# Bucket bits by two signs on ScalarE and a value bias by a one-row product, in a fused attention and feed-forward block

## The chip, the cores and the metric

One core of a Trainium2 chip runs the whole program in one launch. The metric is device time in microseconds, the median over runs; less is better.

## The reference

The input is 16 sequences of 512 tokens with 128 features. Each sequence goes through a layer norm, an attention with 16 heads of 8 features, a second layer norm and a residual, and then a feed-forward network with its own norm and residual. The attention compares queries with queries, and its scores are multiplied by 62, or by 63 where both tokens fall into the same bucket:

```python
q = (x @ Wq.T + bq).reshape(B, S, H, Dh)
v = (x @ Wv.T + bv).reshape(B, S, H, Dh)
proj = einsum('bshe,en->bshn', concat([q, ones]), hyperplanes)   # 6 numbers per token and head
bits = (proj >= 0)
buckets = einsum('bshn,n->bsh', bits, 2 ** arange(6))
scores = einsum('bhsd,bhtd->bhst', q, q) / sqrt(128)
coeff = 62 + (b_hs[:, :, :, None] == b_hs[:, :, None, :])
attn = softmax(scores * coeff)
out = einsum('bhst,bhtd->bhsd', attn, v)
# then: x = x + layernorm(out)
h = silu(x1 @ w1 * s1) * (x1 @ w2 * s2)      # 512 wide
h = gelu(h @ h1 * s3); h = gelu(h @ h2 * s4)
x = x + layernorm(h @ w3 * s5)
```

## The kernel before

The kernel works in turns. A turn i handles the attention of sequence i, and beside it the projections (q, buckets, v) of sequence i+1, the input norm of sequence i+2, and the feed-forward network of sequence i-1 and the end of that of i-2. Turns 2 to 13 carry all of this; turns 0 and 1 have no feed-forward end, turn 14 has no input norm, turn 15 no projection either. Sequence 0's projection stands ahead of turn 0, in a turn of its own without attention.

A turn has 64 slots, one for each attention tile (16 heads by 4 blocks of 128 tokens, 128 by 512 scores each). Every engine walks through the same 64 slots in its own program, and tables of numbers at the head of the file (`BITS_SLOT = 26`, ...) say in which slot of each engine's program a step stands. Each engine runs its program strictly in order and waits on semaphores. So a slot number is a place in an engine's queue, not a time.

A tile goes this way. TensorE multiplies the stacked query parts into one of four score banks (L550). VectorE makes the coefficients of the next tile (L758) and multiplies the scores with the present ones into a ring of 48 tiles in SBUF, with the row maximum beside it (L808). After 8 tiles (a group) VectorE transposes the maxima (L768), and SyncE's queue stores them to DRAM and loads them back as rows on all partitions. GpSimd subtracts the group's logits from them in one instruction of 128 by 4096 (L980), ScalarE takes the exponential in four instructions (L1032), and TensorE multiplies values and probabilities (L570), which for a quad of 16 tiles stand in slots 36 and 38 counted from the quad's first tile. The product of the turn's first quad, in slot 36, is called "the slot-36 product" below. A score product in slot k waits until VectorE is through with tile k-4.

The steps of the change, in before: TensorE projects the queries on the hyperplanes (slot 25, L606). VectorE adds the hyperplane bias and compares with 0, which gives bits of 0 and 1 in bf16 (slot 26, L880). TensorE weighs them with powers of two, once per token (slot 28, L612, copied by ScalarE at L1086) and once as a row (slot 37, L630, copied by ScalarE at L1095). TensorE makes the values in PSUM with four products (slot 32, L619), and VectorE adds the bias, which was loaded as 128 by 512, and writes them to `v_pad` (slot 32, L870). All of these share the bank `aux_bank` with the probability products, so the slot-36 product waits for `v_added` too. ScalarE also writes the first norm of the attention output (L1043, slot 31), for which VectorE waits at L896, and the SiLU (L1150), for which VectorE waits at L907.

## Time and profile before

| | before |
|---|---|
| median of 3 runs | 1383.29 us (1378.63 to 1386.29) |
| profiled execution, first to last instruction | 1378.0 us |
| TensorE busy | 1223.5 us, 89% |
| VectorE busy | 1225.7 us, 89% |
| ScalarE busy | 1084.6 us, 79% |
| GpSimd busy | 1221.7 us, 89% |
| mean granted TensorE clock | 0.975 |

Of the profiled execution only its span is known, 1378.0 us; the fastest of the three runs is 0.6 us above it and the median 5.3 us. Three engines are busy for the same share, so the shares alone don't tell which of them sets the pace: that is read from what ends last in each turn. In this trace a turn is cut at a small memset that VectorE makes in its last slot (L805).

### The profile page before, as it was taken

The page shows a single profiled execution, that of the slowest core. Times are in us where ns is not written, and L with a number is a line of the kernel's source. Part 1 is how long each engine was busy: PE and PEld are TensorE (multiplying, and loading weights), DVE is VectorE, ACT ScalarE, POOL GpSimd, SP SyncE. Part 2 cuts the span into 40 slices and gives each one's busy share as a digit, 9 for nine tenths or more (in the row PEclk, how much of TensorE's full clock was granted, in tenths as well). Part 3 has the DMA queues.
Part 4 walks back from the last instruction along what each step waited for, and adds up shares of the span by engine and source line. Part 5 has one row for each costly group of instructions (what it writes and reads, how often), then busy time and mean ns, then how long its engine had stood idle before and what let it go on. Part 6 is the DMA issues. An engine that isn't in the chain of part 4 may idle for free. (4 is left out here: it accounts for less than half of the span.)

```text
span 1378.0 us, 19641 instructions
## 1 busy us (share of the span) xinstructions
PE 1223.5 (89%) x5302; PEld 500.2 (36%) x5394; DVE 1225.7 (89%) x3837; ACT 1084.6 (79%) x1573; POOL 1221.7 (89%) x259
## 2 busy tenths in 40 slices
PE   3666799999989999998989999998999999898897
PEld 1211234343333434333343434433343433333343
DVE  4988999999999999999999999999999999999420
ACT  2344778979797988979798897979798897979852
POOL 2699999999999999999999999999999998999810
PEclk9877999999999999999999999999999999999998
DMA  3563445444544455455544544454454535453100
GB/s 104 154 182 112 132 111 154 127 130 120 147 120 118 132 134 141 109 140 125 131 133 124 142 123 132 133 139 129 114 136 128 145 98 146 120 135 102 40 8 8
DMA packets 89470, 167.37 MB, mean 121 GB/s; under 512 B 18192, under 2 KB 54160, under 8 KB 89360
## 3 DMA queue, kind: packets, MB, share of 16 engines
q1 hardware_dynamic: 89252, 165.82, 44.6%
q8 instruction: 43, 0.70, 0.2%
q14 instruction: 67, 0.55, 0.1%
q10 hardware_dynamic: 108, 0.30, 0.1%
HBM read 150.59 MB, written 15.47 MB: 121 GB/s over the span
## 5 line engine op out<-in xcount | busy, mean ns | idle before, releaser
L980 POOL TENSOR_TENSOR logits<-max_row,logits 128x4096 f32<-128x4096 f32 x128 | 1138.7, 8915 | 65.6 <-DMA max_row<-max_scratch 41.0
L808 DVE CUSTOM_DVE_ANT_0 logits<-s_bank,coeff 128x512 f32<-128x512 f32 x1024 | 692.5, 676 | 0.0
L1032 ACT ACTIVATE logits<-logits 128x1024 f32<-128x1024 f32 x512 | 509.0, 1048 | 44.8 <-POOL logits L980 43.6
L758 DVE TENSOR_SCALAR coeff<-brow,bcol 128x516 bf16<-128x516 bf16 x1024 | 485.2, 474 | 36.8 <-PE s_bank L550 31.2
L550 PE MATMUL s_bank<-mov_stack,stat_stack 128*128 128x512 bf16 x932 | 324.8, 393 | 42.4 <-DVE rowmax L808 31.7
L570 PE MATMUL aux_bank<-logits,v_pad 128*32 128x512 f32 x2048 | 255.3, 618 | 39.8 <-ACT logits L1032 38.9
L701 PE MATMUL f_bank<-hid_b,h_sb 128*128 128x512 f32 x512 | 249.0, 594 | 0.9
L690 PE MATMUL f_bank<-hid_a,h_sb 128*128 128x512 f32 x512 | 246.1, 592 | 0.1
L550 PEld LDWEIGHTS s_bank<-mov_stack,stat_stack 128*128 128x128 bf16 x1024 | 93.2, 99 | 317.7 <-DVE rowmax L808 177.8
L690 PEld LDWEIGHTS f_bank<-hid_a,h_sb 128*128 128x128 f32 x512 | 96.0, 190 | 80.6 <-issue 69.3
L701 PEld LDWEIGHTS f_bank<-hid_b,h_sb 128*128 128x128 f32 x512 | 95.0, 190 | 80.8 <-issue 70.9
L570 PEld LDWEIGHTS aux_bank<-logits,v_pad 128*32 128x32 f32 x2048 | 56.1, 111 | 183.7 <-issue 142.6
L1032 ACT ACT_TABLE_LOAD x88 | 112.9, 1283 | 1.5
L1052 ACT COPY oT<-aux_bank 128x512 f32<-128x512 f32 x32 | 18.5, 579 | 86.9 <-PE aux_bank L570 86.9
L808 DVE DVE_READ_ACCUMULATOR2_ANT rowmax<- 128x1 f32 x1024 | 84.5, 83 | 0.0
L662 PE MATMUL f_bank<-ynT,w_sb 128*128 128x512 f32 x128 | 68.2, 617 | 16.6 <-ACT ynT L1145 8.4
L676 PE MATMUL f_bank<-ynT,w_sb 128*128 128x512 f32 x128 | 68.5, 617 | 7.2 <-ACT hid_a L1150 6.3
L717 PEld LDWEIGHTS f_bank<-w_sb,hid_a 128*128 128x128 f32 x512 | 63.0, 193 | 20.6 <-issue 16.9
L717 PE MATMUL f_bank<-w_sb,hid_a 128*128 128x128 f32 x512 | 69.0, 283 | 0.9 <-ACT hid_a L1160 0.7
L1155 ACT ACTIVATE hid_b<-f_bank,scales_sb 128x512 f32<-128x512 f32 x64 | 40.5, 684 | 35.7 <-PE f_bank L690 35.5
L907 DVE SCALAR_TENSOR_TENSOR hid_a<-f_bank,scales_sb,hid_a 128x512 f32<-128x512 f32 x64 | 46.6, 748 | 22.5 <-ACT hid_a L1150 15.1
L999 POOL TENSOR_TENSOR ffn<-ffn,y 128x512 f32<-128x512 f32 x16 | 20.6, 1286 | 46.9 <-ACT ffn L1141 46.9
(101 smaller groups left out, 911.5 us busy)
## 6 DMA issues: line engine op xcount, KB each, us to landing
max_row<-max_scratch SPq DMA_DIRECT2D x128, 512.0 KB, 4.2
brow<-bucket_scratch SPq DMA_DIRECT2D x63, 522.0 KB, 6.3
mov_stack<-q_scratch SPq DMA_DIRECT2D x192, 96.0 KB
stat_stack<-q_scratch SPq DMA_DIRECT2D x189, 96.0 KB
max_scratch<-rowmax_T SPq DMA_DIRECT2D x512, 1.0 KB
q_scratch<-q_parts SPq DMA_DIRECT2D x16, 384.0 KB, 4.6
x_in<-in_x SPq DMA_DIRECT2D x16, 256.0 KB, 3.1
q_scratch<-q_parts SPq DMA_DIRECT2D x16, 256.0 KB, 5.1
```

The costliest lines, as they stand in the source:

```text
L550: nc.tensor.matmul(tile_bank(k)[:], stat_stack[:, quad % 2, hh, t * P:(t + 1) * P], mov_stack[:, quad % 2, hh, :], start=True, stop=True). ...
L570: last = nc.tensor.matmul(aux_bank[hh * VW:(hh + 1) * VW, :], values[:, first:first + VW], logits[:, ring(b, quad * QT + hh * ST + j), :], ...
L662: nc.tensor.matmul(f_bank[GATE_BANKS[j]][:], w1_sb[:, col], ynT[:], start=True, stop=True).then_inc(w1_psum, 1)
L676: nc.tensor.matmul(f_bank[UP_BANKS[j]][:], w2_sb[:, col], ynT[:], start=True, stop=True).then_inc(w2_psum, 1)
L690: last = nc.tensor.matmul(f_bank[FIRST_HIDDEN_BANKS[j]][:], h1_sb[:, k, col], hid_a[:, k, :], start=(k == 0), stop=(k == HT - 1))
L701: last = nc.tensor.matmul(f_bank[SECOND_HIDDEN_BANKS[j]][:], h2_sb[:, k, col], hid_b[:, k, :], start=(k == 0), stop=(k == HT - 1))
L717: last = nc.tensor.matmul(f_bank[OUTPUT_BANK][:, t * P:(t + 1) * P], hid_a[:, j, t * P:(t + 1) * P], w3_sb[:, j, :], start=(j == 0), stop= ...
L758: nc.vector.tensor_scalar(coeff[:, k % 3, :].rearrange("p (r n) -> p r n", r=ROW_RUNS), brow[:, h // 4 % 2, h % 4, :, 0:RUN], bcol[:, b % ...
L808: nc.vector.tensor_tensor_reduce(out=logits[:, ring(b, k), :], in0=tile_bank(k)[:], in1=coeff[:, k % 3, 0:SEQ], scale=float(E) ** -0.5, sc ...
L907: nc.vector.scalar_tensor_tensor(out=hid_a[:, j, :], in0=f_bank[UP_BANKS[j]][:], scalar=scales_sb[:, 1, j:j + 1], in1=hid_a[:, j, :], op0= ...
L980: nc.gpsimd.tensor_tensor(tiles, max_row[:, m % 2].unsqueeze(2).broadcast_to([P, GROUP, ST, SEQ]), tiles, ALU.subtract).then_inc(below_max ...
L1032: nc.scalar.activation(logits[:, first:first + 2, :], logits[:, first:first + 2, :], ACT.Exp, scale=-1.0).then_inc(probs_done, 1)
```

## The change

- The bits: ScalarE takes Sign(projection + hyperplane bias), which is -1, 0 or 1, and then Sign(2x + 1), which maps -1 to -1 and 0 and 1 to 1. Where the bits were 0 and 1 they are now -1 and 1: the weighted sums differ, but two tokens have equal sums in the same cases, which is all that the coefficients use. The second instruction waits for the first.
- The value bias: a one-row product (a row of ones by the row `bv`) opens each of the four accumulations, and ScalarE copies the sum to `v_pad`.
- VectorE has neither of the two steps any more. The bias is loaded as 1 by 128 in place of 128 by 512.
- The tables of slots are changed in some twenty places. On SyncE's queue the four stores of a group's maxima (L469) now stand ahead of the store of the query parts (slot 34) and of that of the row of bucket sums (slot 41, L458), behind which they stood before; the load of the maxima stays where it was.

```diff
-OUTPUT_SLOTS = (100, 101, 104, 104)
+OUTPUT_SLOTS = (100, 101, 104, 105)
-BITS_SLOT = 26
+BITS_SLOT = 23
-BCOL_SLOT = 28
+BCOL_SLOT = 29
-ROW_COPY_SLOT = 34
+ROW_COPY_SLOT = 37
-ATT_NORM_SLOT = 31
+ATT_NORM_SLOT = 29
...
-Y1_MOMENTS_SLOT = 32
+Y1_MOMENTS_SLOT = 33
...
-STORE_SLOT = 4
+STORE_SLOT = 1
...
@@ TensorE
                     for t in range(ST):
-                        last = nc.tensor.matmul(projection_bank(p, 1)[:, t * P:(t + 1) * P], xnT[:, t * P:(t + 1) * P], wv_sb[:],
-                                                start=True, stop=True)
+                        values = projection_bank(p, 1)[:, t * P:(t + 1) * P]
+                        nc.tensor.matmul(values, ones_row[:], bv_sb[:], start=True, stop=False)
+                        last = nc.tensor.matmul(values, xnT[:, t * P:(t + 1) * P], wv_sb[:], start=False, stop=True)
@@ VectorE
-                    nc.vector.tensor_tensor(
-                        v_pad[:, p % 2, :, 0:PAD_PITCH - HALF_W].rearrange("p r (h w) -> p r h w", w=VW)[:, :, :, 0:DH],
-                        projection_bank(p, 1)[:].rearrange("p (r h d) -> p r h d", r=2 * ST, d=DH),
-                        bv_sb[:].rearrange("p (r h d) -> p r h d", r=2 * ST, d=DH),
-                        ALU.add).then_inc(v_added, 1)
...
-                    nc.vector.tensor_scalar(bitsT[:], projection_bank(p, 0)[0:NH * H, :], hbias_sb[:], 0.0, ALU.add,
-                                            ALU.is_ge).then_inc(bits_done, 1)
@@ ScalarE
+                if k == V_ADD_SLOT:
+                    act.wait_ge(v_psum, p + 1)
...
+                    nc.scalar.copy(
+                        v_pad[:, p % 2, :, 0:PAD_PITCH - HALF_W].rearrange("p r (h w) -> p r h w", w=VW)[:, :, :, 0:DH],
+                        projection_bank(p, 1)[:].rearrange("p (r h d) -> p r h d", r=2 * ST, d=DH)).then_inc(v_added, 1)
+                if k == BITS_SLOT:
+                    act.wait_ge(proj_psum, p + 1)
...
+                    nc.scalar.activation(bitsT[:], projection_bank(p, 0)[0:NH * H, :], ACT.Sign,
+                                         bias=hbias_sb[:]).then_inc(signs_done, 1)
+                    act.wait_ge(signs_done, p + 1)
+                    nc.scalar.activation(bitsT[:], bitsT[:], ACT.Sign, bias=1.0, scale=2.0).then_inc(bits_done, 1)
```

How this stands in ScalarE's program of a full turn, around slots 22 to 34. Before, from the second GELU's first pair (L1160) to its second pair and the copy of the row (L1095); `logits<-logits` are the exponentials:

```order
L1160 ACTIVATE hid_a<-f_bank,scales_sb 128x512 x2
L1032 ACT_TABLE_LOAD
L1032 ACTIVATE logits<-logits 128x1024
L1038 ACTIVATE x_var<-x_mv,eps 128x4
L1039 ACTIVATE x_shift<-x_mv 128x4
L1038 ACTIVATE att_var<-att_mv,eps 128x4
L1039 ACTIVATE att_shift<-att_mv 128x4
L1086 COPY bcol<-aux_bank 128x64
L1032 ACTIVATE logits<-logits 128x1024 x3
L1043 ACTIVATE f_bank<-att,att_bias,att_rstd 128x128 x4
L1032 ACTIVATE logits<-logits 128x1024
L1160 ACT_TABLE_LOAD
```

The same place of ScalarE's program in the change (its L1161, L1014, L1087 and L1025 are L1160, L1032, L1086 and L1043 of before):

```order
L1161 ACTIVATE hid_a<-f_bank,scales_sb 128x512 x2
L1078 ACTIVATE bitsT<-aux_bank,hbias_sb 96x512
L1081 ACTIVATE bitsT<-bitsT 96x512
L1014 ACT_TABLE_LOAD
L1014 ACTIVATE logits<-logits 128x1024
...
L1087 COPY bcol<-aux_bank 128x64
L1014 ACTIVATE logits<-logits 128x1024 x2
L1025 ACTIVATE f_bank<-att,att_bias,att_rstd 128x128 x4
L1014 ACTIVATE logits<-logits 128x1024 x2
L1070 COPY v_pad<-aux_bank 128x8x8x8
L1161 ACT_TABLE_LOAD
```

Two signs stand ahead of the first exponential, the copy of the values stands behind the last one, and the norm has moved from behind the third of the group's exponentials to behind the second. No table load is added: both programs have 196.

TensorE's program of a full turn from the bucket sums (slot 28 or 29) to the slot-36 product, before (L701 is a product of the second hidden layer, L550 a score product):

```order
L612 MATMUL aux_bank<-weights,bitsT 128x16 x4
L701 MATMUL f_bank<-hid_b,h_sb 128x512
L550 MATMUL s_bank<-mov_stack,stat_stack 128x512 x3
L701 MATMUL f_bank<-hid_b,h_sb 128x512
L550 MATMUL s_bank<-mov_stack,stat_stack 128x512
L619 MATMUL aux_bank<-wv_sb,xnT 128x128 x4
L550 MATMUL s_bank<-mov_stack,stat_stack 128x512 x2
L701 MATMUL f_bank<-hid_b,h_sb 128x512 x2
L550 MATMUL s_bank<-mov_stack,stat_stack 128x512 x2
L570 MATMUL aux_bank<-logits,v_pad 32x512 x8
```

And in the change, from the value products on (L625 is the bias row, L626 the product that was L619, L573 the probability product):

```order
L625 MATMUL aux_bank<-bv_sb,ones_row 128x128
L626 MATMUL aux_bank<-wv_sb,xnT 128x128
...
L625 MATMUL aux_bank<-bv_sb,ones_row 128x128
L626 MATMUL aux_bank<-wv_sb,xnT 128x128
L553 MATMUL s_bank<-mov_stack,stat_stack 128x512 x2
L707 MATMUL f_bank<-hid_b,h_sb 128x512 x2
L553 MATMUL s_bank<-mov_stack,stat_stack 128x512 x2
L573 MATMUL aux_bank<-logits,v_pad 32x512 x8
```

Four one-row products have come in between the value products; what stands between them and the slot-36 product is the same.

## Rows read from the trace of the kernel before

**Rows 1.** The page: span, and busy time of each engine with its share

```profile
span 1378.0 us, 19641 instructions
PE 1223.5 (89%) x5302; PEld 500.2 (36%) x5394; DVE 1225.7 (89%) x3837; ACT 1084.6 (79%) x1573; POOL 1221.7 (89%) x259
```

**Rows 2.** Busy time in stretches: turns 2 to 13, then turns 3, 4, 7

```profile
core 0: us, PE busy (x) PEld busy (x) DVE busy (x) ACT busy (x) POOL busy (x), PEclk, DMA share, GB/s
184.00:1131.20 947.20, 888.41 (x3973) 370.19 (x4044) 913.87 (x2871) 823.08 (x1188) 910.48 (x181) 1.00 0.48 130
262.70:340.80 78.10, 73.92 (x333) 30.79 (x337) 76.03 (x242) 68.39 (x99) 75.74 (x16) 1.00 0.49 131
340.80:421.70 80.90, 75.30 (x333) 31.54 (x337) 76.29 (x240) 68.66 (x99) 76.48 (x16) 0.98 0.49 127
579.20:658.80 79.60, 73.90 (x333) 30.79 (x337) 76.20 (x241) 68.48 (x100) 76.93 (x16) 1.00 0.49 129
```

**Rows 3.** Timeline of turn 3 (start, duration, engine), several engines, mostly left out

```profile
262.74 0.06 DVE L805 MEMSET spare<- 128x1 f32 x1
...
289.45 0.59 ACT L1052 COPY oT<-aux_bank 128x512 f32<-128x512 f32 x1 [4.80 <-PE aux_bank L570]
...
298.31 0.19 ACT L1086 COPY bcol<-aux_bank 128x64 f32<-128x64 f32 x1
...
302.79 1.05 ACT L1032 ACTIVATE logits<-logits 128x1024 f32<-128x1024 f32 x1
...
303.98 1.50 PE L570 MATMUL aux_bank<-logits,v_pad 128*32 128x512 f32 x12 [0.82 <-ACT logits L1032]
...
327.26 0.75 DVE L907 SCALAR_TENSOR_TENSOR hid_a<-f_bank,scales_sb,hid_a 128x512 f32<-128x512 f32 x1 [0.46 <-ACT hid_a L1150]
...
328.37 0.75 DVE L907 SCALAR_TENSOR_TENSOR hid_a<-f_bank,scales_sb,hid_a 128x512 f32<-128x512 f32 x1 [0.36 <-PE f_bank L676]
```

**Rows 4.** Timeline of turn 7, the same places and some more

```profile
616.37 2.95 ACT L1032 ACTIVATE logits<-logits 128x1024 f32<-128x1024 f32 x3 [1.42 <-POOL logits L980]
...
621.95 1.49 PE L570 MATMUL aux_bank<-logits,v_pad 128*32 128x512 f32 x12 [2.33 <-ACT logits L1032]
...
625.53 0.44 ACT L1095 CAST brow<-f_bank 16x344 bf16<-16x344 f32 x1 [1.14 <-PE f_bank L630]
...
629.01 0.48 DVE L758 TENSOR_SCALAR coeff<-brow,bcol 128x516 bf16<-128x516 bf16 x1 [0.17 <-PE s_bank L550]
```

**Rows 5.** Groups by form: busy us, mean ns of one, idle before

```profile
L550 PE MATMUL s_bank<-mov_stack,stat_stack 128*128 128x512 bf16 x932 | 324.8, 393 | 42.4 <-DVE rowmax L808 31.7 <-DMA mov_stack<-q_scratch 5.0 <-issue 4.8
L1052 ACT COPY oT<-aux_bank 128x512 f32<-128x512 f32 x32 | 18.5, 579 | 86.9 <-PE aux_bank L570 86.9
L880 DVE TENSOR_SCALAR bitsT<-aux_bank,hbias_sb 96x512 bf16<-96x512 f32 x15 | 11.2, 743 | 0.0
L1071 ACT ACTIVATE q_parts<-aux_bank,bq_sb 128x512 bf16<-128x512 f32 x16 | 10.8, 675 | 4.4 <-PE aux_bank L596 4.4
L870 DVE TENSOR_TENSOR v_pad<-aux_bank,bv_sb 128x512 f32<-128x512 f32 x15 | 10.2, 682 | 0.0
L630 PE MATMUL f_bank<-bitsT,weights 96*16 96x512 bf16 x16 | 6.3, 396 | 1.9 <-issue 0.3
```

**Rows 6.** Timeline: the value products of turn 3, and a slower slot-36 product

```profile
299.53 1.05 PE L619 MATMUL aux_bank<-wv_sb,xnT 128*128 128x128 f32 x8
...
383.30 2.45 PE L570 MATMUL aux_bank<-logits,v_pad 128*32 128x512 f32 x16 [2.07 <-ACT logits L1032]
```

**Rows 7.** Timeline of the first 30 us, from the hyperplane product on

```profile
15.59 2.02 PE L606 MATMUL f_bank<-qT,hyper_sb 128*96 128x512 f32 x2 [1.36 <-ACT qT L1075]
...
19.13 0.72 DVE L880 TENSOR_SCALAR bitsT<-f_bank,hbias_sb 96x512 bf16<-96x512 f32 x1
...
20.10 2.05 PE L619 MATMUL f_bank<-wv_sb,xnT 128*128 128x128 f32 x8
...
28.61 2.40 PE L550 MATMUL s_bank<-mov_stack,stat_stack 128*128 128x512 bf16 x5 [4.96 <-DMA mov_stack<-q_scratch]
```

More of the change, by code:

```diff
@@ L89 @@
 LATE_X_PREPARE_SLOT = 38
-X_RSTD_SLOT = 40
+X_RSTD_SLOT = 41
 LATE_X_RSTD_SLOT = 47
@@ L94 @@
 XNT_SLOT = 57
-Q_COPY_SLOT = 57
-Q_SLOT = 59
+Q_COPY_SLOT = 56
+Q_SLOT = 61
 Q_HIGH_SLOT = 56
@@ L108 @@
 ROW_SLOT = 37
-ROW_COPY_SLOT = 34
+ROW_COPY_SLOT = 37
 ATT_STATS_SLOT = 24
 ATT_MOMENTS_SLOT = 25
-ATT_PREPARE_SLOT = 27
-ATT_RSTD_SLOT = 32
-ATT_NORM_SLOT = 31
+ATT_PREPARE_SLOT = 24
+ATT_RSTD_SLOT = 33
+ATT_NORM_SLOT = 29
 RESIDUAL_SLOT = 32
 Y1_STATS_SLOT = 32
-Y1_MOMENTS_SLOT = 32
+Y1_MOMENTS_SLOT = 33
 Y1_PREPARE_SLOT = 34
@@ L126 @@
 END_SUM_SLOT = 42
-END_PREPARE_SLOT = 49
+END_PREPARE_SLOT = 50
 END_RSTD_SLOT = 56
@@ L143 @@
 FIRST_Q_STORE_SLOT = 30
-X_LOAD_SLOT = 1
+X_LOAD_SLOT = 0
 ROW_STORE_SLOT = 41
@@ L174, in sandwich_kernel @@
         bq_sb = sb("bq_sb", [P, 1])
-        bv_sb = sb("bv_sb", [P, ST * E])
+        bv_sb = sb("bv_sb", [1, E])
+        ones_row = sb("ones_row", [1, P])
         hyper_sb = sb("hyper_sb", [P, NH * H])
@@ L250, in sandwich_kernel @@
         stacks_clear = sem("stacks_clear")
+        ones_made = sem("ones_made")
         v_pad_clear = sem("v_pad_clear")
@@ L268, in sandwich_kernel @@
         weights_made = sem("weights_made")
+        signs_done = sem("signs_done")
         bits_done = sem("bits_done")
@@ L617, in project_step @@
                         pe.wait_ge(bcol_done, p + 1)
+                    if not begun(p):
+                        pe.wait_ge(ones_made, 1)
                     for t in range(ST):
-                        last = nc.tensor.matmul(projection_bank(p, 1)[:, t * P:(t + 1) * P], xnT[:, t * P:(t + 1) * P], wv_sb[:],
-                                                start=True, stop=True)
+                        values = projection_bank(p, 1)[:, t * P:(t + 1) * P]
+                        nc.tensor.matmul(values, ones_row[:], bv_sb[:], start=True, stop=False)
+                        last = nc.tensor.matmul(values, xnT[:, t * P:(t + 1) * P], wv_sb[:], start=False, stop=True)
                     last.then_inc(v_psum, 1)
@@ L962, in _ @@
             nc.gpsimd.memset(eps[:], EPS).then_inc(consts_made, 1)
+            nc.gpsimd.memset(ones_row[:], 1.0).then_inc(ones_made, 1)
             pool.wait_ge(consts_made, 1)
@@ L1080, in project_step @@
             def project_step(p, k):
+                if k == V_ADD_SLOT:
+                    act.wait_ge(v_psum, p + 1)
+                    if p > 1:
+                        act.wait_ge(pv_psum, (p - 1) * QUADS)
+                    if p == 0:
+                        act.wait_ge(v_pad_clear, 2)
+                    nc.scalar.copy(
[3 more added lines that the diff above has]
+                    act.wait_ge(proj_psum, p + 1)
+                    if begun(p):
+                        act.wait_ge(brow_psum, p)
+                    nc.scalar.activation(bitsT[:], projection_bank(p, 0)[0:NH * H, :], ACT.Sign,
+                                         bias=hbias_sb[:]).then_inc(signs_done, 1)
+                    act.wait_ge(signs_done, p + 1)
+                    nc.scalar.activation(bitsT[:], bitsT[:], ACT.Sign, bias=1.0, scale=2.0).then_inc(bits_done, 1)
                 if k == BCOL_COPY_SLOT:
```

18 lines of the change are left out of this document (2 added, 16 removed).

## The prediction

> **What bounds the kernel now.** I read the page first [rows 1]. VectorE, TensorE and GpSimd are each busy for 89% of 1378.0 us, so no share names the bound. The table of stretches comes next [rows 2]: the twelve full turns 2 to 13 take 947.2 us, 78.93 each, and hold 913.87 us of VectorE (76.2 a turn), 910.48 of GpSimd (75.9), 888.41 of TensorE (74.0) and 823.08 of ScalarE (68.6). VectorE is idle for only 2.8 us a turn. By that alone, what is taken from VectorE comes back in full.
>
> The timeline says less. The turns are not equal: turn 3 takes 78.1 us, turn 7 79.6, turn 4 80.9, with the same work [rows 2]. I looked for the event that moves with the end of the turn. It is the slot-36 product. In turn 3, which starts at 262.74, it begins at 303.98 [rows 3], 41.2 us into the turn, and the turn ends (340.80) 36.8 us later. In turn 7 it begins at 621.95 [rows 4], 42.75 us into it, and the turn ends (658.80) 36.85 us later. So a turn is "slot-36 product plus 36.8". The reason is in the rows behind it: eight us later VectorE waits 0.17 us for a score bank (629.01) [rows 4], because TensorE must get through slots 36 to 38 before it makes that score.
>
> What holds the slot-36 product? TensorE waits for ScalarE's exponentials in both turns, 0.82 and 2.33 us [rows 3, 4]. In turn 7 ScalarE had itself waited 1.42 us for GpSimd (616.37) [rows 4]. In turn 3 it had not: from its copy at 289.45, for which it waited 4.80 us, ScalarE runs without a gap to the end of the last exponential at 303.84 [rows 3]. So even in the quickest turn ScalarE, at 79% the least busy engine, sets the slot-36 product, through a stretch of 14.4 us in which it has no slack. VectorE has 0 to 0.17 us there. Two chains of equal length end at the same place.
>
> **The change part by part.**
>
> *VectorE.* The comparison is 0.743 us and the bias 0.682 [rows 5], with no idle time ahead of either, 1.43 us a turn. Both stand ahead of the place where VectorE waits for TensorE.
>
> *The two signs.* No Sign is in the trace. The nearest rows are a bias activation from PSUM to bf16, 0.675, and a copy, 0.579 [rows 5]; the bounds of a sign are these two. I take 0.675 for both, since both have a bias, and 0.04 for the wait between them: 1.39 us (1.2 by the lower bound). The Trainium skill (ScalarE: Activation LUTs, "What ACT_TABLE_LOAD costs") says that the per-element time is the same for every function, and that a pointer operand adds about 93 ns; the trace agrees, its two rows are 96 ns apart. The signs stand ahead of the first of the group's exponentials, in the stretch without slack. In turn 3 all 1.39 count. In turn 7 the 1.42 us that ScalarE waited for GpSimd swallows them.
>
> *The value copy.* Some 0.58 us by the copy's row [rows 5]; its lower bound is 0.49, since the exponential ahead overlaps with what follows it (1.05 long [rows 3], where three in a row take 2.95 [rows 4]). It stands behind the last exponential, and the slot-36 product waits for it, since they share the bank. VectorE's bias add was done long before. So +0.5 us in every turn.
>
> Together the slot-36 product moves from 41.2 to 43.1 in turn 3 (1.39 + 0.5) and from 42.75 to 43.25 in turn 7. All turns now have it at 43.1 to 43.3, whether GpSimd is late or not. Before, the mean turn had 78.93 - 36.8 = 42.1. The mean shift is 1.1 us, of which GpSimd's lateness has paid 0.8.
>
> *The one-row products.* Four of them cost what the value products cost, 1.05 us a turn [rows 6]. Nothing in the trace has one row; its nearest pair, 96 rows at 396 ns and 128 rows at 393 [rows 5], shows no saving with fewer rows, so I take the full price and zero as the other bound. In a full turn it costs nothing: TensorE arrives 0.82 us or more before the exponentials in before [rows 3], and these are now 1.9 us later in that turn, so 1.7 us of cover are left after 1.05; without the cover the price would be 12.6 us over twelve turns. The values also wait for the copy of the bucket sums, which comes 1.4 us later; it ended at 298.50 [rows 3] and the values began at 299.53 [rows 6], so 1.0 of that was slack and 0.4 goes off the cover. The Trainium skill (TensorE: Matmul & The Clock Gate, "Why this matters for your kernels") has it that a product over 32 rows takes as long as one over 128; by that rule the head costs what I write below, and 2.05 less if time went with rows.
>
> *What gives back.* In turn 3 VectorE comes 1.9 us later to its waits in slot 52, where it waited 0.46 us for ScalarE's SiLU and 0.36 for TensorE [rows 3]. These waits go if ScalarE's chain to there moved by less. It did: ScalarE waited 1.14 us for the row of bucket sums (625.53) [rows 4], and with the copy moved to slot 37 it has three more steps to do first. ScalarE's chain is later by 1.39 + 0.5 - 1.14 = 0.75, at most 1.1 where TensorE's transposes hold it. So VectorE's 1.9 become 1.9 - 0.46 - 0.36 = 1.08. The norm for VectorE's residual is one exponential earlier; VectorE reaches it 0.65 earlier and waits there, which ends ahead of the slot-36 product and counts for nothing.
>
> So turn 3 goes from 78.1 to 79.15, and with all turns alike the mean goes from 78.93 to about 79.15: +0.2 a turn, +2.6 over turns 2 to 14.
>
> *SyncE's queue.* The maxima's stores no longer stand behind the row's store, which now comes later, so its delay holds up none of them. The q store (two issues) now stands ahead of one load of maxima a turn; that load waits for its stores to land anyway. Nothing.
>
> *Head.* The signs can start when the projection ends (15.59 + 2.02 = 17.61) and end at 19.04, where VectorE's comparison ended at 19.85: -0.8. The value products took 2.05 us at the lower of the clock's two levels and now take 4.1. Behind them come the row, its copy, and the loads for which the first scores waited 4.96 us [rows 7]: +1.25.
>
> *Turns 0 and 1* have little ScalarE work, so VectorE's 1.43 may come back, 0 to 2.9 us in the two; I take 1.0.
>
> The sum is 2.6 + 1.25 - 1.0 = +2.9 us, on the profiled 1378.0 gives 1380.9 (x 1.002). The median of the runs is 5.3 above that span; there it gives 1386.
>
> **The rivals.**
>
> *VectorE's time comes back.* It has the most work and the least idle time [rows 2]. Then 15 turns by 1.43 give -21.4, with the head -20: 1363. Against it: ScalarE's gapless stretch in turn 3. Chance 0.12. A part of it, -0.6 a turn, needs signs and copy to cost 0.7 less together, or a chain that starts earlier: 1375, chance 0.13.
>
> *Slower: the waits in slot 52 don't give back.* If ScalarE's chain to the SiLU moves with the slot-36 product, because the transposes or the second moments hold it, VectorE still waits 0.46 and 0.36 there, and a turn is 43.2 + 36.8 = 80.0: +1.07 by 13 turns, with the head +14: 1397. It decides from the point where that chain is later by more than 1.5 us. Chance 0.17.
>
> *Slower: TensorE's clock.* In turn 4 TensorE waited 2.07 us, and the product behind it took 2.45 us [rows 6], with a granted clock of 0.98 for the turn, which was 80.9 long [rows 2]. If TensorE's idle time gathers ahead of the slot-36 product, more turns look so: +1.9 in each, 1405. Chance 0.07; by my count it waits 1.2 us there, less than now.
>
> [...]
>
> **How the numbers follow.** My forecast, within 0.5%, has 0.51. Half a per cent, 6.9 us, is about what a measurement of this kernel can tell from no change. Faster: 0.12 + 0.13 = 0.25. Slower: 0.17 + 0.07 = 0.24. The time is 1386; its own range, from the bounds of the signs (0.4 us a turn), of the copy and of turns 0 and 1, is 1379 to 1393. Both signs hold much, so the range goes from 1366 to 1400, which leaves out the full return and the clock.
>
> **What would show it.** Right: the slot-36 product at 43.0 to 43.4 us in all full turns, ScalarE without a gap ahead of it, waiting nowhere for GpSimd in slots 29 to 32; VectorE's idle time up from 2.8 to about 4.3 us a turn, in new waits of 1.4 us for the norm (its residual add) and over 1 us for a score bank behind the slot-36 product; no waits for the SiLU in slot 52; signs of 0.65 to 0.70. Wrong: a slot-36 product at or ahead of 42, which would say that the signs or the copy are hidden; or waits of 0.46 and 0.36 still in slot 52; or granted clocks under 0.99 in several turns.

## The result and the profile after

The changed kernel takes 1400.18 us (median of 4 runs, 1398.38 to 1404.81) against 1382.51 us for the kernel before (4 runs, 1378.63 to 1386.29): a ratio of 1.0127, with a 95% interval of 1.0092 to 1.0161. It is slower. The forecast was 1386. The profiled execution took 1404.81 us, with a span of 1403.0, 25.0 more than before. That execution is the slowest of the changed kernel's four, and before's profiled one is the fastest of its four: the medians are only 17.7 us apart, so some 7 of the 25.0 us are differences between executions of one kernel.

The page, in the lines that answer to [rows 1]:

```profile
span 1403.0 us, 20006 instructions
PE 1286.4 (92%) x5522; PEld 530.8 (38%) x5522; DVE 1207.3 (86%) x3805; ACT 1111.0 (79%) x1621; POOL 1221.6 (87%) x260
```

VectorE is busy for 18.4 us less; the steps taken away held 21.4 [rows 5] and 1.4 for sequence 0, and its other instructions take some 4 more. TensorE is busy for 62.9 us more. Some 10 of these are no work of the change: the trace of before has 5302 of TensorE's instructions, and e12 below, which runs the same ones, has 5394 and is busy for 1233.4 us, so 92 records are missing in before. The rest is for four one-row products a turn and for the lower clock shown below. The table of stretches, for turns 2 to 13, then turns 3, 4 and 8:

```profile
188.90:1158.20 969.30, 933.45 (x4142) 391.80 (x4140) 900.22 (x2847) 842.00 (x1224) 909.19 (x181) 0.99 0.48 127
267.80:347.30 79.50, 76.70 (x347) 32.23 (x345) 75.02 (x239) 70.12 (x102) 74.64 (x15) 1.00 0.46 129
347.30:431.80 84.50, 80.06 (x347) 33.77 (x345) 75.23 (x240) 70.24 (x103) 77.81 (x17) 0.96 0.47 125
673.70:753.50 79.80, 76.61 (x347) 32.18 (x345) 74.91 (x239) 70.13 (x102) 74.35 (x16) 1.00 0.50 129
```

Twelve full turns take 969.3 us where they took 947.2 [rows 2], 22.1 of the 25.0. They are far less equal: 78.8 to 84.5 us, where they were 78.1 to 80.9. The last three columns hold the key; the first of them is the granted clock, 1.00 in turn 3 and 0.96 in turn 4. So I looked at turn 4 in pieces of 5 us:

```profile
380.00:385.00 5.00, 4.47 (x18) 1.85 (x17) 5.00 (x17) 4.94 (x6) 5.00 (x1) 1.00 0.33 105
385.00:390.00 5.00, 3.83 (x15) 2.37 (x12) 2.58 (x9) 4.99 (x13) 4.25 (x4) 0.80 0.15 49
390.00:395.00 5.00, 5.00 (x12) 2.62 (x12) 3.92 (x15) 3.86 (x5) 5.00 (x1) 0.51 0.93 248
395.00:400.00 5.00, 5.00 (x35) 2.26 (x34) 2.95 (x8) 4.42 (x7) 4.27 (x6) 1.00 0.78 172
```

From 388 to 395 TensorE has its lower clock, 1.2 GHz (0.51 in the third row). This is what TensorE does there:

```profile
386.82 0.48 PE L625 MATMUL aux_bank<-bv_sb,ones_row 1*128 1x128 f32 x2 [1.17 <-ACT bcol L1087]
...
389.52 0.80 PE L626 MATMUL aux_bank<-wv_sb,xnT 128*128 128x128 f32 x2
...
391.55 1.06 PE L553 MATMUL s_bank<-mov_stack,stat_stack 128*128 128x512 bf16 x2
...
395.87 1.92 PE L573 MATMUL aux_bank<-logits,v_pad 128*32 128x512 f32 x16
```

It waits 1.17 us for the copy of the bucket sums, begins the bias and value products, and within them the clock falls; the slot-36 product comes 9.05 us after their start. In turn 3 the same instructions run at the full clock:

```profile
305.52 0.48 PE L625 MATMUL aux_bank<-bv_sb,ones_row 1*128 1x128 f32 x2 [0.74 <-ACT bcol L1087]
...
305.93 0.30 PEld L626 LDWEIGHTS aux_bank<-wv_sb,xnT 128*128 128x128 f32 x2
305.94 0.49 PE L626 MATMUL aux_bank<-wv_sb,xnT 128*128 128x128 f32 x2
...
308.75 0.59 PE L553 MATMUL s_bank<-mov_stack,stat_stack 128*128 128x512 bf16 x2
...
311.43 1.07 PE L573 MATMUL aux_bank<-logits,v_pad 128*32 128x512 f32 x8
```

The 16 instructions take 3.23 us from the first to the next score product (305.52 to 308.75). Before, eight took 0.89 by the same count (the row of 1.05 us in [rows 6] starts at 299.53, and the next score product at 300.42). So each takes 0.20 us instead of 0.11. The slot-36 product follows 5.91 us after their start.

Cut into stretches of 1 us, the trace has a fall of the clock in six of the twelve full turns (4, 6, 7, 9, 11, 12): the first stretch with a lower clock begins 40.4 to 41.4 us into the turn, just behind or in the value products. Before, it fell in one, turn 4. With the fall, the slot-36 product comes 7.6 us after the start of the value products (9.1 in turns 4 and 12), without it 5.9. How long TensorE had waited for the bucket sums does not tell which turns these are: it waited 1.16 us in turn 8, which has no fall, and 0.17 us in turn 9, which has one.

The head runs at the lower clock as well, in both kernels. The traces have no record of the granted clock there, and a table of stretches shows 1.00; but the durations tell it: 0.60 us for the product of the row (L636), whose mean over the whole of before was 0.396 (L630) [rows 5]. The head after:

```profile
19.32 0.79 PE L625 MATMUL f_bank<-bv_sb,ones_row 1*128 1x128 f32 x2
...
20.04 0.80 PE L626 MATMUL f_bank<-wv_sb,xnT 128*128 128x128 f32 x2
...
25.10 0.60 PE L636 MATMUL f_bank<-bitsT,weights 96*16 96x512 bf16 x1
...
31.87 2.40 PE L553 MATMUL s_bank<-mov_stack,stat_stack 128*128 128x512 bf16 x5 [5.20 <-DMA mov_stack<-q_scratch]
```

The value products take 5.78 us there against 1.99 before (20.10 to 22.09). They start 0.78 us earlier (19.32), and the first score product starts at 31.87 instead of 28.61 [rows 7].

The groups that answer to [rows 5] and to VectorE's waits:

```profile
L890 DVE SCALAR_TENSOR_TENSOR hid_a<-f_bank,scales_sb,hid_a 128x512 f32<-128x512 f32 x64 | 46.6, 749 | 13.8 <-ACT hid_a L1151 9.2 <-PE f_bank L682 2.5
L626 PE MATMUL aux_bank<-wv_sb,xnT 128*128 128x128 f32 x120 | 33.3, 364 | 0.0
L625 PE MATMUL aux_bank<-bv_sb,ones_row 1*128 1x128 f32 x120 | 32.6, 355 | 7.1 <-ACT bcol L1087 7.1
L879 DVE TENSOR_TENSOR y<-f_bank,x_res 128x512 f32<-128x512 f32 x16 | 11.1, 692 | 22.6 <-ACT f_bank L1025 22.6
L1078 ACT ACTIVATE bitsT<-aux_bank,hbias_sb 96x512 bf16<-96x512 f32 x15 | 10.2, 677 | 0.9 <-PE aux_bank L609 0.9
L1081 ACT ACTIVATE bitsT<-bitsT 96x512 bf16<-96x512 bf16 x16 | 10.1, 630 | 0.5
L1070 ACT COPY v_pad<-aux_bank 128x512 f32<-128x512 f32 x15 | 8.5, 567 | 3.2 <-PE aux_bank L626 3.2
```

VectorE's waits in turn 3 (its whole list there between the norm and slot 52):

```profile
308.91 0.69 DVE L879 TENSOR_TENSOR y<-f_bank,x_res 128x512 f32<-128x512 f32 x1 [1.52 <-ACT f_bank L1025]
316.31 0.48 DVE L764 TENSOR_SCALAR coeff<-brow,bcol 128x516 bf16<-128x516 bf16 x1 [0.53 <-PE s_bank L553]
318.49 0.48 DVE L764 TENSOR_SCALAR coeff<-brow,bcol 128x516 bf16<-128x516 bf16 x1 [1.09 <-PE s_bank L553]
```

And ScalarE in turn 8, from GpSimd's logits to the copy of the values:

```profile
701.90 2.95 ACT L1014 ACTIVATE logits<-logits 128x1024 f32<-128x1024 f32 x3 [0.89 <-POOL logits L962]
...
707.32 0.68 ACT L1078 ACTIVATE bitsT<-aux_bank,hbias_sb 96x512 bf16<-96x512 f32 x1
708.03 0.63 ACT L1081 ACTIVATE bitsT<-bitsT 96x512 bf16<-96x512 bf16 x1
...
711.50 0.19 ACT L1087 COPY bcol<-aux_bank 128x64 f32<-128x64 f32 x1
...
716.93 0.56 ACT L1070 COPY v_pad<-aux_bank 128x512 f32<-128x512 f32 x1
```

From here on a turn is cut in three: up to the start of the value products, from there to the slot-36 product, and the rest. In all full turns after, the rest is 35.9 us (before, 36.8 in ten of twelve). Without a fall of the clock the middle is 5.9. So what varies is the start of the value products (37.0 to 39.5), and the clock.

### The profile page after: what moved, and what is told of

It reads as the page before. It is cut to its first block and busy times, and to the rows that moved or that the text cites. A ratio compares the mean times of both kernels' runs of the same rounds, so it can differ in the third digit from the quotient of the medians.

```text
span 1403.0 us, 20006 instructions
## 1 busy us (share of the span) xinstructions
PE 1286.4 (92%) x5522; PEld 530.8 (38%) x5522; DVE 1207.3 (86%) x3805; ACT 1111.0 (79%) x1621; POOL 1221.6 (87%) x260
## 3 DMA queue, kind: packets, MB, share of 16 engines
q1 hardware_dynamic: 89110, 165.56, 44.4%
## 5 line engine op out<-in xcount | busy, mean ns | idle before, releaser
L1014 ACT ACTIVATE logits<-logits 128x1024 f32<-128x1024 f32 x512 | 509.8, 1048 | 53.3 <-POOL logits L962 52.1
L553 PE MATMUL s_bank<-mov_stack,stat_stack 128*128 128x512 bf16 x1024 | 353.6, 397 | 33.6 <-DVE rowmax L814 26.9
L573 PE MATMUL aux_bank<-logits,v_pad 128*32 128x512 f32 x2048 | 254.0, 615 | 14.2 <-ACT logits L1014 14.2
L707 PE MATMUL f_bank<-hid_b,h_sb 128*128 128x512 f32 x512 | 256.4, 610 | 0.5 <-ACT hid_b L1156 0.5
L707 PEld LDWEIGHTS f_bank<-hid_b,h_sb 128*128 128x128 f32 x512 | 99.0, 196 | 91.5 <-issue 78.6
L573 PEld LDWEIGHTS aux_bank<-logits,v_pad 128*32 128x32 f32 x2048 | 54.6, 111 | 159.3 <-issue 124.3
```

The costliest lines, as they stand in the source:

```text
L553: nc.tensor.matmul(tile_bank(k)[:], stat_stack[:, quad % 2, hh, t * P:(t + 1) * P], mov_stack[:, quad % 2, hh, :], start=True, stop=True). ...
L573: last = nc.tensor.matmul(aux_bank[hh * VW:(hh + 1) * VW, :], values[:, first:first + VW], logits[:, ring(b, quad * QT + hh * ST + j), :], ...
L707: last = nc.tensor.matmul(f_bank[SECOND_HIDDEN_BANKS[j]][:], h2_sb[:, k, col], hid_b[:, k, :], start=(k == 0), stop=(k == HT - 1))
L1014: nc.scalar.activation(logits[:, first:first + 2, :], logits[:, first:first + 2, :], ACT.Exp, scale=-1.0).then_inc(probs_done, 1)
```

## The experiments

My theory after the result: TensorE loses twice. Each change between products of 1 row and of 128 rows costs it about 0.18 us, since the next weights are not loaded beside the running product (in turn 3 the load of L626 and its product start together, at 305.93 and 305.94); and this thin stretch, with the waits around it, brings the clock down, which costs the turn. The Trainium skill (TensorEngine Tiling (Array Packing), "Key Properties") says that a change of the tiling mode drains TensorE. Whether 1 row after 128 is such a change no run here shows. The first rival is the slower one of the prediction: ScalarE's longer chain costs the time. The second is that adding a second product onto the same columns is what is slow. The table sums up the traces, one profiled execution each; "values" is from the first bias or value product to the next score product, "wait" is TensorE's ahead of the slot-36 product, "falls" are full turns in which the clock falls in or behind the value products or at the slot-36 product. The experiments ran in three batches, and each ratio is to runs of the kernel before in the same batch (medians 1378.80 us for e1 to e4, 1380.08 for e5 to e8, 1379.44 for e9 to e12).

| kernel | values, us | wait, us | falls | turns 2 to 13, us | ratio to before (95%) |
|---|---|---|---|---|---|
| before | 0.89 | 0.8 to 2.3 | 1 | 947.2 | 1 |
| the change | 3.23 | none | 6 | 969.3 | 1.0127 (1.0092 to 1.0161) |
| e1 128-row bias | 1.89 | 1.22 | 0 | 952.3 | 1.0030 (1.0012 to 1.0047) |
| e2 half the changes of rows | 2.66 | 0.45 | 3 | 953.3 | 1.0089 (1.0062 to 1.0117) |
| e3 no bias products | 0.99 | 2.11 | 4 | 960.5 | 1.0093 (1.0073 to 1.0112) |
| e4 before, with one-row products | 3.23 | none | 6 | 971.1 | 1.0213 (1.0192 to 1.0233) |
| e5 one wide row | 2.05 | 1.06 | 1 | 950.8 | 1.0026 (1.0004 to 1.0048) |
| e6 rows spread over slots | 3.67 | none | 4 | 962.6 | 1.0125 (1.0086 to 1.0165) |
| e7 signs alone | 0.99 | 1.69 | 0 | 947.2 | 0.9990 (0.9967 to 1.0013) |
| e8 value half, 128-row bias | 1.79 | 0.4 to 1.6 | 0 | 940.1 | 0.9960 (0.9935 to 0.9985) |
| e9 value half, one-row bias | 3.23 | none to 0.3 | 3 | 957.1 | 1.0087 (1.0056 to 1.0118) |
| e10 wide row twice | 2.90 | 0.20 | 5 | 957.8 | 1.0098 (1.0062 to 1.0134) |
| e11 wide, 128 rows, twice | 2.71 | 0.40 | 0 | 956.9 | 1.0033 (1.0012 to 1.0055) |
| e12 slots alone | 0.89 | 0.9 to 2.1 | 1 | 941.3 | 0.9950 (0.9932 to 0.9969) |

In e6 the 3.67 us end with the last pair and hold two score products.

### e1: the bias product with 128 rows

```diff
-        bv_sb = sb("bv_sb", [1, E])
-        ones_row = sb("ones_row", [1, P])
+        bv_sb = sb("bv_sb", [P, E])          # 128 copies
+        ones_row = sb("ones_row", [P, P])    # filled with 1/128
```

> As the change, but the bias product has 128 rows (all ones divided by 128, against 128 copies of the bias) in place of one row; 16 instructions of TensorE as in the change. Theory: a change between products of 1 row and of 128 rows keeps the next weights from being loaded beside the running product, 0.18 us for each of the 8 changes; then the 16 instructions take 1.8 us instead of 3.2, at the higher clock, and with them go most of the clock dips behind the value products: 1384 to 1391 us. Rival 1: the second product of an accumulation waits for the first on the same columns of the bank: still 3.2 us, 1400. Rival 2: the sequence gets shorter, but the clock falls from the wait for ScalarE's copy ahead of it: still dips in five or more full turns, 1394 to 1399.

Measured: 1382.92 us, 1.0030, just below the range of the theory (1384 to 1391) and far from both rivals. The same 16 instructions, from the timeline of its turn 3, and then its turns 2 to 13:

```profile
300.67 0.49 PE L625 MATMUL aux_bank<-bv_sb,ones_row 128*128 128x128 f32 x2 [0.66 <-ACT bcol L1087]
...
300.88 0.30 PEld L626 LDWEIGHTS aux_bank<-wv_sb,xnT 128*128 128x128 f32 x2
300.99 0.39 PE L626 MATMUL aux_bank<-wv_sb,xnT 128*128 128x128 f32 x2
...
302.55 0.59 PE L553 MATMUL s_bank<-mov_stack,stat_stack 128*128 128x512 bf16 x2
...
306.52 1.06 PE L573 MATMUL aux_bank<-logits,v_pad 128*32 128x512 f32 x8 [1.23 <-ACT v_pad L1070]
```

```profile
184.30:1136.60 952.30, 904.89 (x4141) 381.83 (x4140) 898.82 (x2846) 841.85 (x1225) 909.27 (x181) 1.00 0.48 129
```

1.88 us in place of 3.23, with the same adding onto the same columns: the rows do it, not the accumulation. The load of the weights now starts 0.11 us ahead of its product (300.88 and 300.99), beside the product that is running. The 1.35 us that this saves don't move the slot-36 product at full clock: it follows the start of the values by 5.85 us here and by 5.91 in the change, since it waits 1.23 us for ScalarE's copy. What goes is the fall of the clock, in all full turns, and turns 2 to 13 are 17.0 us shorter. ScalarE's chain is the change's here too, so the first rival is out. This one pair of runs holds most of the answer.

### e2: the same products, half the changes of rows

```diff
-                        nc.tensor.matmul(values, ones_row[:], bv_sb[:], start=True, stop=False)
-                        last = nc.tensor.matmul(values, xnT[:, t * P:(t + 1) * P], wv_sb[:], start=False, stop=True)
+                        pair = [(ones_row[:], bv_sb[:]), (xnT[:, t * P:(t + 1) * P], wv_sb[:])]
+                        for n, (a, b) in enumerate(pair if t % 2 else pair[::-1]):
+                            last = nc.tensor.matmul(values, a, b, start=(n == 0), stop=(n == 1))
```

> As the change, the same eight products (16 instructions), ordered values, row, row, values, twice over, so that 4 changes of the row count are left of 8. Theory of the row-count change: 3.2 - 4 x 0.18 = 2.5 us, 1391 to 1397. Rival, the accumulation onto the same columns: still 3.2 us, since each pair still writes the same columns, 1400.

Measured: 1388.71 us, faster than both expectations (1391 to 1397, and 1400). The values take 2.66 us, and the four changes left cost (2.66 - 1.89)/4 = 0.19 us each over e1. The change has eight, but the first of them lies ahead of the first product, where e1 has a wait in its place; the other seven cost (3.23 - 1.89)/7 = 0.19 as well. Products and columns are the same, so the number of changes is what costs. Against the rival the values got shorter. The clock falls in three full turns. The profiled execution is one of the quick ones of this kernel (1383.4 of span), so its 953.3 us say less than the median.

### e3: no bias products

```diff
-                        nc.tensor.matmul(values, ones_row[:], bv_sb[:], start=True, stop=False)
-                        last = nc.tensor.matmul(values, xnT[:, t * P:(t + 1) * P], wv_sb[:], start=False, stop=True)
+                        last = nc.tensor.matmul(values, xnT[:, t * P:(t + 1) * P], wv_sb[:], start=True, stop=True)
```

> As the change, but without the four bias products, so the values have no bias (the output is not the reference's). Signs, copy and tables are those of the change. If TensorE's stretch of value products is what was mis-sized, it is 0.9 us long, clock dips are left in two full turns or fewer, the first memset is at 102 us, and the time is 1380 to 1388, my forecast or a little less. Rival: ScalarE's longer chain and the new slots cost the time (the slower rival of the prediction): 1394 to 1400 still, with the slot-36 product at 43.2.

Measured: 1392.2 us, which neither theory had. The head is as expected (first memset at 101.5). TensorE has less work than in e1, and the kernel is 9 us slower: in four full turns the clock falls, now at the slot-36 product, behind a wait of 2.11 us, here in turn 2, and then turns 2 to 13:

```profile
227.38 2.54 PE L573 MATMUL aux_bank<-logits,v_pad 128*32 128x512 f32 x16 [2.11 <-ACT v_pad L1069]
```

```profile
183.10:1143.70 960.60, 900.73 (x4046) 373.31 (x4044) 899.21 (x2847) 841.96 (x1224) 909.84 (x181) 0.99 0.48 128
```

So the one-row products are not needed for the fall; idle time does it too. Idle time alone doesn't tell the turn either: TensorE waits 2.11 or 2.12 us there in all twelve full turns, and the clock falls in four. In the turns without a fall the slot-36 product stands where it stands in e1, 5.85 us after the values. The bias product with 128 rows pays for itself by keeping TensorE busy.

### e4: the kernel before, with one-row products added

```diff
+                        nc.tensor.matmul(values, ones_row[:], bv_sb[0:1, 0:P], start=True, stop=True)
                         last = nc.tensor.matmul(values, xnT[:, t * P:(t + 1) * P], wv_sb[:], start=True, stop=True)
```

> The kernel before with four one-row products put ahead of its value products, whose result is overwritten by them; nothing else is touched, VectorE adds the bias. If TensorE's waits for the exponentials (0.8 to 2.3 us) cover it: head +3 only, 1386. If the 2.3 us are more than the cover in the shorter turns: the slot-36 product moves by up to 1.5 us there, +0.7 a turn, and with the head 1395. If the clock adds its dips too: 1398 to 1404, with dips in four or more full turns right behind the value products.

Measured: 1407.42 us, beyond the upper expectation. In turns without a fall the slot-36 product is at 42.8, with TensorE not waiting at all, where the mean was 42.0: here the cover is used up and 0.8 us more is paid. Six full turns have the fall, at 39.7 to 41.1 us. Signs and new slots have no part in it, and neither has a wait ahead of the value products: TensorE had one in only one of the six (0.76 us in turn 4). Turns 2 to 13:

```profile
192.00:1163.00 971.00, 935.80 (x4141) 389.69 (x4140) 915.21 (x2869) 823.04 (x1188) 910.16 (x181) 0.99 0.47 127
```

### e5: one wide row

```diff
-                        nc.tensor.matmul(values, ones_row[:], bv_sb[:], start=True, stop=False)   # four times, 128 columns
+                    nc.tensor.matmul(projection_bank(p, 1)[:], ones_row[:], bv_sb[:], start=True, stop=False)   # once, 512
```

> As the change, but one bias product of 1 row by 512 columns opens the whole bank, and the four value products add to it: 2 changes of the row count in place of 8, 10 instructions. Theory of the row-count change: 0.87 for the wide product (a value product costs 0.22 for 128 columns), 0.89 for the values and 2 x 0.18, 2.1 us in all. If a one-row product counts as activity for the clock, it behaves as the 128-row one: no dips in the full turns, 1383. If it counts for nothing, TensorE is idle for the clock for longer than without any bias product: dips in four or more full turns, 1390 to 1397.

Measured: 1383.94 us, values of 2.05 us (2.1 expected), one fall. As good as the 128-row bias, with two changes of rows left. Of the two theories on record this is the result of the first, that one-row columns keep the clock up as those of 128 rows do; e10 below is against it.

### e6: the pairs spread over slots

```diff
-                if k == V_SLOT:
+                if k in VALUE_SLOTS:          # (32, 33, 34, 34)
...
-                    for t in range(ST):
+                    for t in [n for n in range(ST) if VALUE_SLOTS[n] == k]:
```

> As the change, with the four pairs of bias and value products spread over TensorE's slots 32, 33, 34 and 34, between score products and the hidden layer's products; the same instructions and the same number of row-count changes. If the clock falls because the thin stretch is in one piece: dips in two full turns or fewer, 1383 to 1388. If it falls for the total of thin work in the turn or for the one-row products as such: dips in five or more full turns, 1397 to 1404.

Measured: 1395.67 us, with falls in four full turns, between the two expectations. Spreading the same products between dense ones helps little or nothing (turns 2 to 13 are 6.7 us shorter than the change's in the one traced execution, but the ratios, 1.0125 and 1.0127, are the same). Inconclusive on the form of the thin stretch; moving the products by these few us at least did not help the median.

### e7, e8, e9: the halves of the change

e7 takes the value bias back to VectorE; e8 and e9 take the bits back to VectorE (slot 26), e8 with the 128-row bias, e9 with the one-row bias as in the change. All have the change's other slots.

```diff
@@ e7, VectorE
+                    nc.vector.tensor_tensor(
+                        v_pad[:, p % 2, :, 0:PAD_PITCH - HALF_W].rearrange("p r (h w) -> p r h w", w=VW)[:, :, :, 0:DH],
+                        projection_bank(p, 1)[:].rearrange("p (r h d) -> p r h d", r=2 * ST, d=DH),
+                        bv_sb[:].rearrange("p (r h d) -> p r h d", r=2 * ST, d=DH),
+                        ALU.add).then_inc(v_added, 1)
@@ e8 and e9, VectorE
+                    nc.vector.tensor_scalar(bitsT[:], projection_bank(p, 0)[0:NH * H, :], hbias_sb[:], 0.0, ALU.add,
+                                            ALU.is_ge).then_inc(bits_done, 1)
```

> The first half of the change alone: bits by two signs on ScalarE, the slots of the change; the value bias stays on VectorE (bias 128 by 512) and there is no one-row product. Theory (the slot-36 product stands at the end of ScalarE's exponentials): 0.57 less than with the copy, 42.4 where it is 42.9 to 43.4, a turn of 78.9: 1377 to 1382; TensorE waits 1.5 us there, so a dip in up to three full turns adds 2 each, 1384. Rival: VectorE's 0.68 a turn comes onto the path again, since what follows the slot-36 product is VectorE's work: 79.5 a turn, 1386 to 1390.

> The second half alone, with the 128-row bias product: value bias on TensorE, copy by ScalarE, bits of 0 and 1 on VectorE (slot 26), the other slots of the change. ScalarE has 1.35 us less ahead of its first exponential. Theory: the slot-36 product at 41.6 to 42.2, a turn of 78.1 to 78.4, 1368 to 1374. Rival: VectorE's comparison waits for TensorE's projection or is on the path: no gain, 1378 to 1383.

> The second half of the change alone, with its one-row products as they are: value bias by TensorE, copy by ScalarE, bits of 0 and 1 on VectorE (slot 26), the other slots of the change. Against the run with the 128-row bias and bits on VectorE, only the number of rows differs. Theory: the value products take 3.2 us instead of 1.8 and this is still nearly covered at full clock (slot-36 product at 42.5 instead of 42.4), the head is 1.3 longer, and clock dips come in five or more full turns, 1.9 each: 1388 to 1397. Rival: the dips need ScalarE's longer chain ahead of the values (the wait for the copy of the bucket sums), which is gone here: two dips or fewer, 1375 to 1380.

Measured: e7 1378.83, e8 1375.15, e9 1391.77 us. Turns 2 to 13 of e7, e8 and e9:

```profile
184.00:1131.20 947.20, 894.56 (x4046) 371.11 (x4044) 906.12 (x2859) 834.80 (x1212) 909.72 (x181) 1.00 0.49 130
```

```profile
185.10:1125.20 940.10, 901.82 (x4141) 382.86 (x4140) 903.05 (x2857) 828.38 (x1200) 909.42 (x181) 1.00 0.49 131
```

```profile
191.30:1148.40 957.10, 926.18 (x4142) 389.02 (x4140) 904.30 (x2858) 828.77 (x1200) 909.66 (x181) 0.99 0.48 128
```

The signs alone leave the kernel where it was, as the theory had it (1377 to 1382); no full turn has a fall. The value half alone is 0.4% faster with 128 rows and 0.9% slower with one, with everything else equal: the number of rows is worth 1.3%. Not all of that is the clock. Of the 17.0 us between the two stretches the three falls are 5.1 (1.7 each); some 6 are cover that is used up, since without a fall the slot-36 product follows the start of the values by 5.9 us in e9 (6.2 in two turns) and by 5.4 in the mean in e8; some 6 are values that start later, half of that in turn 6. e8 is slower than expected (1368 to 1374), since the slot-36 product is at 41.7 to 43.6 and not at 41.6 to 42.2. e9 has three falls in the full turns behind the values, one in turn 14 and one in turn 6 earlier in the turn, where five or more were expected; the median is as expected. The rival (two or fewer, 1375 to 1380) falls, but with the shorter chain the falls are fewer.

### e10 and e11: the wide product twice, of 1 row and of 128

```diff
+                    nc.tensor.matmul(projection_bank(p, 1)[:], ones_row[:], bv_sb[:], start=True, stop=True)
                     nc.tensor.matmul(projection_bank(p, 1)[:], ones_row[:], bv_sb[:], start=True, stop=False)
```

e11 is this with `bv_sb` and `ones_row` of 128 rows, as in e1.

> As the run with one wide one-row product, which is issued twice (the first result is overwritten by the second): value products of 2.9 us, about as long as in the change, with 2 changes of the row count in place of 8. If a stream of one-row columns keeps the clock up, no more dips than with the wide product once (1), 1384 to 1388. If the clock falls for it as for idle time: five or more dips in the full turns, 1394 to 1402.

> The same with 128 rows (ones divided by 128 against 128 copies of the bias): 2.7 us of value products, all of 128 rows, no change of the row count. In both theories no dips in the full turns; TensorE is busy up to the slot-36 product, which ScalarE still sets: 1383 to 1387, of which 0.8 over the 128-row run with four small products is the head. Rival: what matters is that TensorE is 0.9 or more us later with the values, whatever their rows: a turn 0.5 longer, 1390.

Measured: e10 1393.0, e11 1385.11 us: e10 just below the range of its second theory (1394 to 1402), e11 as expected. The stretches of turns 2 to 13, e10 and then e11:

```profile
190.70:1148.40 957.70, 925.00 (x4093) 382.60 (x4092) 899.24 (x2845) 841.87 (x1224) 909.86 (x181) 0.99 0.48 128
```

```profile
185.20:1142.00 956.80, 916.54 (x4093) 380.20 (x4092) 898.73 (x2845) 841.91 (x1224) 911.18 (x182) 1.00 0.49 128
```

Nearly the same length of value products (2.90 and 2.71 us), without a gap longer than a change of rows: five falls with one row, none with 128 (e11's only fall is in turn 6, at 24.5 us, and that turn is 82.6 us long). In these two executions the clock falls behind one-row products, and not behind products of 128 rows of about the same length. But the stretches of turns 2 to 13 are nearly equal. From the start of the values to the slot-36 product e10 takes 7.1 us more in all, for its falls; but in e11 the values start later, 38.0 us into the turn in the mean against 37.5, which takes 6.0 of it back, half of that in turn 6. Of the 6.9 us between the two spans 5.5 lie ahead of turn 2 (first memset at 105.9 and 104.8, and turn 1 has 84.8 and 80.4 us). So the medians, 7.9 us apart, show that the rows cost time, and the traces that the clock falls; that the one is the price of the other is not shown by this pair. Nor do e5 and e10 agree on what a one-row product is to the clock: one more of them takes the falls from one to five, and why is open. That their values take 0.8 to 1.0 us longer than e1's doesn't show at full clock: in both the slot-36 product follows by 5.85 us, as there. The change of rows behind the wide products costs 0.19 us as well (2.90 - 2.71); the one ahead of them falls into the wait.

### e12: the slots alone

The kernel before with the slots of the change, and the comparison in its slot 26. Some of the lines:

```diff
-BCOL_SLOT = 28
+BCOL_SLOT = 29
-ROW_COPY_SLOT = 34
+ROW_COPY_SLOT = 37
-ATT_NORM_SLOT = 31
+ATT_NORM_SLOT = 29
-STORE_SLOT = 4
+STORE_SLOT = 1
```

> The kernel before with the slots of the change and nothing else (bits and bias on VectorE, the comparison in its slot 26). If the 0.9 us between slot-36 product and the end of a turn (36.8 before, 35.9 after) came from the slots, above all the later copy of the row: the slot-36 product at 41.2 to 42.2, a turn of 77.4 to 78.1, 1366 to 1373, and it beats both kernels. Rival: they came from VectorE's 1.43 us, or VectorE, busy for 76.2 us of a turn, becomes the bound: 78.9 a turn, 1378 to 1383.

Measured: 1373.85 us, 0.9950 (0.9932 to 0.9969), faster than both kernels. Its turns 2 to 13:

```profile
187.40:1128.80 941.40, 895.00 (x4046) 371.21 (x4044) 909.68 (x2871) 821.72 (x1188) 909.28 (x181) 1.00 0.50 130
```

The rest of a turn is 36.0 to 36.1 us in eight of its full turns and up to 37.5 in the others, where it was 36.8: the slots bring most of the 0.9 by themselves. The time is just above the expected 1366 to 1373: the slot-36 product is where it was, at 41.3 to 43.1, and not at 41.2 to 42.2 throughout. The changed arithmetic, against its own slots, costs 1.0127/0.9950 = 1.018.

## Why the prediction was wrong

**What the 25.0 us are.** Head and turn 0 +3.9 (first memset at 106.2 instead of 102.3), turn 1 +1.0. Turns 2 to 13 +22.1: e1, which has the change without falls of the clock, has +5.1 there, and the other 17.0 are what e1 does without. Of these, 13.1 are the falls, measured directly, as the time by which the slot-36 product comes later than 5.91 us after the values (1.7 in four turns, 3.1 and 3.2 in two). The other 3.9 are mostly value products that start later than in e1, above all in turns 4 and 12 (39.5), where ScalarE waited 1.6 and 1.3 us for GpSimd. That GpSimd was late there because of the clock is not shown: turn 3, ahead of turn 4, has no fall, and in e1, which has no fall in any full turn, the values of turn 10 start at 38.6. Behind turn 13, -2.0.

**The step that failed** is the paragraph on the one-row products: "Four of them cost what the value products cost, 1.05 us a turn" and "In a full turn it costs nothing". The size was wrong: 2.34 us a turn, of which seven changes of rows at 0.19 are 1.34 (3.23 - 1.89). The cover held all the same: at full clock the slot-36 product is at 42.9 to 43.9, TensorE being done just as ScalarE is. What failed is "costs nothing": I asked only whether TensorE would be late, not what its clock would be after a stretch of thin work. e1 against the change shows it, with only the rows changed: no fall against six. e8 against e9 and e10 against e11 agree in the falls (none against three, none against five), with the reservations made there.

**The rival "Slower: TensorE's clock"** (0.07, 1405) had the right cost and the right sign, granted clocks under 0.99 in several turns, but not the right condition. It wanted idle time to gather ahead of the slot-36 product, and I gave it little because "by my count it waits 1.2 us there, less than now". TensorE does not even wait there any more. The thin work had moved ahead, into the value products themselves; the waits of 0.2 to 1.2 us for the bucket sums ahead of them are not needed for it (e4). Its 1405 comes close to the 1404.81 of the profiled execution by luck: it counted +1.9 in each further turn that falls, and the median is 1400.18. What decides in which turns the clock falls stays open. The Trainium skill (TensorE: Matmul & The Clock Gate, "HAM oscillation — how this bites in real kernels") tells how waits for DMA between bursts of products bring the clock down, in a kernel whose waits are 3 to 5 us. e3 agrees in kind, with shorter waits than the page's (2.11 us, four falls). In the change and in e4 it falls with no wait ahead of the slot-36 product at all.

**The head**: +1.25 forecast, of which -0.8 for the signs (right: the value products start 0.78 us earlier) and +2.05 for the rows, which were +3.8. The first score product starts 3.26 us later.

**The signs and the copy** were priced right: 0.677 and 0.630 for 0.675 each, and 0.567 for 0.58. Alone on the same slots the signs cost 5.9 us over twelve turns (947.2 - 941.3), 0.5 a turn, and 0.4% by the ratios (0.9990/0.9950).

**The slot-36 product** at 43.0 to 43.4 "in all full turns": without falls it is at 42.9 to 43.9, mean 43.4, in the change, and 42.9 to 44.4 in e1, mean 43.5. The low end is right. Before, the mean was 42.0, so e1 has it 1.5 us later, where I had 1.1. GpSimd's lateness is not swallowed: it now comes ahead of the signs (0.89 us at 701.90 in turn 8), where they cannot hide it.

**What gives back**: forecast 0.82, measured 36.8 to 35.9, 0.9, in every full turn; the rival without it falls. (The wait for the score bank that I placed eight us behind the slot-36 product comes 7.1 us behind it, 629.01 - 621.95.) In slot 52 VectorE no longer waits for ScalarE, and 0.15 us for TensorE where it was 0.36. e12 shows that the slots do most of this without any change in VectorE's work. I had put it down to the row's copy and the delay together; and that the slots alone would make the kernel before faster by 0.5% I did not draw from it.

**VectorE's time** did not come back, as forecast: 4.5 us idle in turn 3 (79.5 - 75.0; forecast 4.3), with waits of 1.52, 0.53 and 1.09 us where 1.4 and over 1 were named.

**The sum without the clock.** In e1, which has no falls in the full turns, the change is at 1.0030 (1.0012 to 1.0047) where I had 1.002. So the forecast, within 0.5%, holds for the mechanism that it modelled, and that was not the one that decided.

## What to carry to other kernels

A product that adds a bias to TensorE's accumulation should have the row count of its neighbours, or be one wide product: the same sum with 128 rows was 1.0% quicker in the change (1.0127/1.0030) and 1.3% in its value half (1.0087/0.9960). e10 warns that a longer one-row product loses the advantage again. When work is moved to a covered place on TensorE, look at the clock in stretches of a few us ahead of and behind it, not only at whether the wait covers it. And measure slots and arithmetic apart: the slots of this change were worth 0.5%, and the arithmetic took 1.8% back.

## What the runs showed of the hardware

- A change between fp32 products of 1 row and of 128 rows takes TensorE 0.19 us at the full clock (3.23, 2.66 and 1.89 us with 7, 4 and 0 changes behind the first of the same 16 instructions). At a change the next weights are not loaded ahead of their product (the change: 305.93 and 305.94; e1: 300.88 and 300.99). In the head, at the lower clock, the 16 take 5.78 us.
- A product of 1 row takes as long as one of 128 rows: the first of the two wide ones (512 columns) is followed by the second after 0.96 us with 1 row and with 128 (turn 3 of e10, 308.19 to 309.15, and of e11, 302.63 to 303.59). The clock fell behind such products more often than behind those of 128 rows: six full turns against none (the change and e1), three against none (e9, e8), five against none (e10, e11), one profiled execution each.
- Removing work from TensorE made the kernel slower: without the bias products 1392.2 us, with 128-row ones 1382.9 (e3, e1).
